# Relative-position attention layer: the stores of the relative products move from SP's queue to ACT's, behind ACT's copies

## The reference

```python
q, k, v = ...                       # (8, 16, 512, 16), from layernorm(x) and from the context
QEr  = jnp.einsum('bhsd,ld->bhsl', q, Er_s)      # 512 x 512 for each head
padded   = jnp.pad(QEr, ((0, 0), (0, 0), (0, 0), (1, 0)))
Srel     = padded.reshape(B, H, C + 1, R)[:, :, 1:, :]
attn = (QK + Srel) / math.sqrt(dh)
attn = jnp.where(causal[None, None], attn, -jnp.inf)
attn = jax.nn.softmax(attn, axis=-1)
out  = jnp.einsum('bhqk,bhkd->bhqd', attn, v)
x = x + out
```

## Time and profile before

| | us |
|---|---|
| median of 3 runs | 4367.12 |
| lowest and highest | 4364.86 and 4370.69 |
| the profiled execution's own time | 4376.57 |
| its span | 4374.7 |
| busy: PE, DVE, ACT, POOL | 3537.7, 2556.5, 1760.6, 1149.3 |
| this layer's attention, first transfer to last score | about 2210 to 3125 |

### The profile page before, as it was taken

How to read it: one execution, slowest core, us unless ns; L and a number is a source line. 1 busy time by engine, 2 the same in 40 slices (tenths; PEclk the granted TensorE clock), 3 DMA queues, 4 the chain that set the end, 5 groups by cost and what they waited for, 6 DMA issues and landing times. The chain is left out here.

```text
span 4374.7 us, 68566 instructions
## 1 busy us (share of the span) xinstructions
PE 3537.7 (81%) x18821; PEld 1770.6 (40%) x18821; DVE 2556.5 (58%) x7436; ACT 1760.6 (40%) x2506; POOL 1149.3 (26%) x1239
## 2 busy tenths in 40 slices
PE   3999999897399899969957777776538999996697
PEld 1343343343133333336634444444313434335465
DVE  4665665776487777853125555555666666663531
ACT  0454455443044344441125545555433445552111
POOL 2334430001445444401022222221222212201132
PEclk7999999898699999979978888888658999996799
DMA  5543540001454344310048888888332432313133
GB/s 109 84 68 62 77 73 12 19 1 42 72 93 83 74 83 78 73 46 0 0 104 223 231 231 220 232 232 229 125 56 35 56 49 35 49 16 107 46 99 68
DMA packets 211868, 392.82 MB, mean 90 GB/s; under 512 B 24624, under 2 KB 76688, under 8 KB 211360
## 3 DMA queue, kind: packets, MB, share of 16 engines
q1 hardware_dynamic: 205344, 379.99, 39.9%
q0 software_dynamic: 6144, 8.39, 1.1%
HBM read 189.88 MB, written 96.47 MB: 65 GB/s over the span
## 5 line engine op out<-in xcount | busy, mean ns | idle before, releaser
L424 DVE CUSTOM_DVE_ANT_0 A_sums<-A_p_ps,A_bias 128x512 bf16<-128x512 f32 x1536 | 1006.1, 687 | 411.8 <-PE A_p_ps L270 389.4
L497 ACT ACTIVATE A_probs<-A_p_ps 128x1024 f32<-128x1024 f32 x640 | 654.3, 1024 | 613.0 <-PE A_p_ps L289 591.0
L270 PE MATMUL A_p_ps<-A_k_stack,A_q_stack 96*128 96x512 bf16 x1536 | 512.0, 390 | 106.5 <-DVE A_nmax L424 96.4
L284 PE MATMUL A_p_ps<-A_q_stack,A_k_stack 99*128 99x512 bf16 x1536 | 461.9, 382 | 0.1
L299 PE MATMUL A_oT_ps<-A_probs,A_v_aug 128*17 128x512 f32 x3072 | 407.0, 602 | 3.2 <-ACT A_probs L497 2.4
L1082 DVE CUSTOM_DVE_ANT_0 A_scores<-A_qk_ps,A_rel_in 128x384 f32<-128x384 f32 (+3 forms) x512 | 232.7, 486 | 215.6 <-POOL A_rel_in L1151 114.8
L990 PE MATMUL A_t_ps<-ident,A_scores 128*128 128x128 f32 x1280 | 225.3, 315 | 134.5 <-DVE A_probsT L1072 124.7
L270 PEld LDWEIGHTS A_p_ps<-A_k_stack,A_q_stack 96*128 96x128 bf16 x1536 | 135.6, 98 | 486.1 <-DVE A_nmax L424 387.6
L289 PE MATMUL A_p_ps<-A_biasT,ident_bf 128*128 128x512 bf16 x1024 | 307.4, 381 | 0.0
L1072 DVE COPY A_probsT<-A_t_ps 128x1024 f32<-128x1024 f32 (+3 forms) x256 | 210.5, 822 | 120.7 <-PE A_t_ps L990 114.1
L1133 ACT ACTIVATE A_scores<-A_scores,A_nmax 128x384 f32<-128x384 f32 (+3 forms) x512 | 257.9, 555 | 48.5 <-DVE A_nmax L1082 48.3
(11 more groups left out here) (356 smaller groups left out, 5901.6 us busy)
## 6 DMA issues: line engine op xcount, KB each, us to landing
A_k_stack<-A_parts SPq DMA_DIRECT2D x192, 256.0 KB, 8.9
A_q_stack<-A_parts SPq DMA_DIRECT2D x192, 256.0 KB, 9.2
A_rel_dram<-A_rel_out SPq DMA_DIRECT2D x64, 512.0 KB, 4.9
A_rel_in<-A_rel_dram SPq DMA_DIRECT2D x64, 512.0 KB
A_rel_dram<-A_rel_out SPq DMA_DIRECT2D x64, 384.0 KB, 4.4
A_rel_in<-A_rel_dram SPq DMA_DIRECT2D x64, 384.0 KB, 4.4
A_ctxT<-in_ctxT SPq DMA_DIRECT2D x32, 512.0 KB, 12.7
A_mask_in<-in_mask SPq DMA_DIRECT2D x64, 256.0 KB, 3.5
```

Source lines behind the costliest of these rows:

```text
L270: nc.tensor.matmul(p1_ps[i % 2][:, :], q_stack[0:KS, a_par, j * GH + i, t * P:(t + 1) * P], k_stack[0:KS, a_par, j * GH + i, :], start=Tru ...
L284: last = nc.tensor.matmul(p2_ps[half][:, i % 2, :], k_stack[:, par, j * GH + i, kb * P:(kb + 1) * P], q_stack[:, par, j * GH + i, :], star ...
L424: nc.vector.tensor_tensor_reduce(out=sums[:, i % NX, :], in0=p1_ps[i % 2][:, :], in1=bias[:, t, :], scale=-1.0, scalar=3.4028235e38, op0=A ...
L497: nc.scalar.activation(dst, src, ACT.Exp).then_inc(exp_done, 1)
```

## The change

The function that issued both stores of a step on SP is gone; a function of the same waits and the same transfer issues one store on ACT, at the end of each position, behind the exponentials. SP's frame keeps loads, stack and context transfers in the order they had. No buffer, semaphore, size or other order changes.

```diff
+        def act_rel_store(act, b, a, h):
+            _, _, n = block_of(a)
+            act.wait_ge(rel_copied, (b * STEPS + a) * 2 + h + 1)
+            if later(b * STEPS + a - NI + 1):
+                act.wait_ge(rel_loaded[a % NI][h], (b * (STEPS // NI) + a // NI) * 16)
+            act.dma_start(bass.AP(rel_dram, a % NI * RING + h * RING // 2, [[2 * n, P], [1, 2 * n]]),
+                          rel_out[a % NO][:, 2 * h * n:(2 * h + 2) * n]).then_inc(rel_stored[a % NO][h], 16)
...
                         nc.scalar.activation(scores[u % NP][:, i, 0:n], scores[u % NP][:, i, 0:n], ACT.Exp,
                                              bias=nmax[:, u % NP, i:i + 1], scale=-1.0).then_inc(exp_done, 1)
+                if has(b, a):
+                    act_rel_store(act, b, a, half)
...
-        def sp_rel_store(sp, b, a):
-            _, _, n = block_of(a)
-            for h in range(2):
-                sp.wait_ge(rel_copied, (b * STEPS + a) * 2 + h + 1)
-                if later(b * STEPS + a - NI + 1):
-                    sp.wait_ge(rel_loaded[a % NI][h], (b * (STEPS // NI) + a // NI) * 16)
-                sp.dma_start(bass.AP(rel_dram, a % NI * RING + h * RING // 2, [[2 * n, P], [1, 2 * n]]),
-                             rel_out[a % NO][:, 2 * h * n:(2 * h + 2) * n]).then_inc(rel_stored[a % NO][h], 16)
...
                 if has(b, s + LEAD - 1):
                     sp_rel_load(sp, b, s + LEAD - 1)
-                if has(b, s + LEAD):
-                    sp_rel_store(sp, b, s + LEAD)
                 if after and s in (0, 1):
```

## The result

| | before | after |
|---|---|---|
| median of 4 runs, us | 4365.99 (4363.15 to 4370.69) | 4222.56 (4217.24 to 4229.22) |
| profiled execution's own time, us | 4376.57 | 4223.41 |
| its span, us | 4374.7 | 4221.6 |
| granted TensorE clock over the span | 0.895 | 0.915 |
| the eight frames of the layer, us | 837.6 | 686.7 |

The changed kernel takes 0.9671 of the time [0.9654, 0.9688]. In the profiled executions 150.9 of the 153.1 us of span come out of the eight frames of this layer, so the rest of the program needs no look.

A forecast was written before the change was run, and what follows sets the result against it. SP's in-order chain of load, store and landing was taken to bound the kernel, as long as a step (6.8 us). Terms -50 - 20 - 10 + 18 = -62 us gave 4305 us at the median; range 4255 to 4390.

The forecast's parts named there:

- the term for PE (context and clock): PE's 25.9 us of waits for the next context, 10 us taken as gained; nothing counted for a faster PE clock.
- the mask: DVE's 74.9 us of waits for the mask, without the layer's filling: 50 us taken as gained.
- ACT's issues: ACT issues 256 stores; bounds nothing and 154 us, a third of 57 us taken as cost: +18 us.
- the root: DVE's waits for POOL's root (L1142), 27.9 us in 6 waits: 20 us taken as gained.
- The three terms: DVE's waits for mask and root and PE's waits for the context, forecast at -50, -20 and -10 us.
- The first rival: DMA transfers are the bound, so early loads only wait inside the DMA engines: 4367 us, chance 0.10.
- the slower rival: ACT becomes the bound, all 256 issues on the path at 0.60 us: +51 us, 4418 us, chance 0.16.
- the context: PE's waits for the next context's transfer in SP's queue, 25.9 us in 6 waits: 10 us taken as gained.
- I count nothing for that: Fewer waits may raise PE's granted clock, 0.82 to 0.87 in these frames; sized at nothing.
- the ceiling: All three waits go, up to 97 us in six frames and about 11 in the last: 4259 us, chance 0.10.
- a sign to look for: SP's waits for stores to land fall from 470.7 us to below 100; SP waits for DVE's scores instead.
- The other signs: Mask waits about 25 us, root below 10, steady frame about 99 at share above 0.90, PE's copy waits up under 20.

The follow-up runs named there:

- the spare stores: Changed kernel with every store issued a second time, to a DRAM buffer that nothing reads: 4299.36 us, ratio 0.9847.
- the early context in the kernel before: Kernel before, stores on SP, with the next context's transfer moved from step 6 to step 5, ahead of the stack transfers: 4379.7 us, ratio 1.0027.
- the one-step kernel: Changed kernel whose loads also wait until DVE has scored one step before their own, instead of four: 4503.3 us, ratio 1.0308.

## Why the prediction was right and wrong

The forecast gave 62 us, the eight profiled frames gave 150.9, 89 more. Of these, 40 are the term for PE (context and clock), 23 the mask, 18 ACT's issues, 1 the root, and 6 other waits that the sum left out. The three terms at their full bounds, 74.9 + 27.9 + 25.9 = 128.7 us, would have given 4238 us, still above what was measured.

**Right: the mechanism and its sign.** The chain load, landing, next store, landing held the layer. Undoing it on one queue gives 131 of the 143 us, and a longer wait in front of the load takes it all back. The first rival (transfers are the bound) fell with this. The Trainium skill ("DMA: Bandwidth & Descriptors", section "Issuing engines are not separate DMA queues") says that transfers started by different engines run on the same 16 DMA engines. The runs agree as far as they go, since one queue carried 276 GB/s in a frame for which two queues show 274. It also says that starting them on several engines saves only the issuing time. That does not describe this change; what was saved is the time that ready stores stood behind a waiting load.

**Right: the root.** -20 forecast, -21.0 measured. The direction has its reason; that it came to within 1 us is luck, since no row stood behind taking 20 of 27.9.

**Right: ACT is not the bound**, the slower rival. Its point of decision was 0.31 us uncovered per issue. 256 further issues cost 0.04 us each, at most 0.10.

**Mis-sized: the mask.** -50 forecast, -73.1 measured. The step that failed is to count only 15 of the 40 us of waits behind the stack transfers as gained. The 40 was sound, though 6.72 us was not the longest wait: the trace has seven, one in each of frames 0 to 6, 41.9 us in all and up to 7.83 us. That 25 of the 40 would stay was not. I argued that the engines were full there because their share was 0.90 to 1.09, where they moved 183 to 281 GB/s. Over the same 26.6 us they moved 227 GB/s before, 277 after and 326 with the spare stores, so over the burst they were not full. An average lead of 7.2 us more, with no lead under 8.9 us, left 1.8 us of mask waits. I had also expected up to 12 us more, from one step.

**Mis-sized: the context, and the line "I count nothing for that", said of the clock.** This is the largest step that failed. -10 forecast, -50.4 measured. PE's wait of 25.9 us went altogether, and DVE's waits for products of PE fell by 38.5 and 11.9 us. PE's busy time fell by 55.8 us with the same matmuls, as this group shows, before and then after (busy us, mean ns, idle before it):

```profile
L927 PE MATMUL A_front_ps<-A_ctxT,A_wk 128*128 128x512 f32 x48 | 33.7, 841 | 25.9 <-DMA A_ctxT<-in_ctxT 25.9
```

```profile
L927 PE MATMUL A_front_ps<-A_ctxT,A_wk 128*128 128x512 f32 x48 | 24.3, 631 | 0.1
```

How the 50 us split between a context that comes in time and a faster PE is not settled: no run holds the clock and moves the context. That the products can come earlier at an unchanged clock is shown by the early context in the kernel before (85.4 to 33.3 us, clock 0.896 over the span against 0.895), but there DVE was held up by masks at the same time (121.1 us), so PE had more time to get ahead.

**Mis-sized: ACT's issues.** +18 forecast, and nothing of it is seen: PE's waits for ACT's copies go from 4.0 to 7.1 us, and DVE's waits have no term for it. No run isolates the 256 issues, so 0 is the reading of these waits and not a measurement. Of the two reasons given for the lower bound, waits in front of copies and exponentials that still run, it is the second: the issue runs under exponentials that were already handed over. I had expected the store some 2 us after the copy, and it leaves 0.1 us after it. Placed where nothing covers it, it cost 21 us.

**Wrong: the ceiling.** "A steady frame holds 0.85 x 108.2 = 92 us of DMA work" is the step that put 4222 out of the range. It made frames under 92 us impossible, and they take 80.9 to 94.1. The same bytes need (232 GB/s x 106.0 us) / 359 GB/s = 68.5 us at the rate of the spare stores' run. The six frames gave 118.5 us instead of at most 97. The ceiling also left out frame 0, which gave 20.0 us, from 104.2 to 84.2; the last frame gave 12.4 for the 11 allowed.

**Wrong: a sign to look for.** SP's waits for landings were to fall below 100 us with waits for DVE's scores in their place; 427.6 us remain, and 15.8 us are for scores. By this sign a theory that holds would have been refuted. What a queue's wait means depends on whether it is ahead of or behind its consumers. The other signs came: the root below 10 us, the share of a steady frame at 0.90 to 0.99, PE's waits for copies up by less than 20.

The terms as measured, -73.1 - 21.0 - 38.5 - 11.9 and others -6.4, make the 150.9 us of the profiled layer.

## What to carry to other kernels

For each transfer on a busy queue, measure the time from when its data is ready to its issue, and from its issue to its first use; a store that stands ready behind a waiting load is worth moving, and swapping two blocks on the same queue may be nearly all of it. Do not take a DMA share as a capacity: turn it into GB/s and set it beside the highest rate that a run with such transfers shows. And put an issue behind instructions whose conditions are already met, so that it runs under them.

## What the runs showed of the hardware

An issue on ACT takes 0.33 us at the median and ran under an exponential, 0.14 us after the copy before it ended, though it stands behind two exponentials in the program: the queue side of ACT is ahead of its arithmetic. Placed directly behind the copy it left a gap of 0.62 us. The DMA engines moved 359 GB/s in a frame at a share of 1.05, and 357 at 0.93, so nearly equal rates can have different shares. PE's granted clock was higher where there were fewer waits: 0.82 to 0.87 in the frames of the earlier trace rows, 0.90 to 0.96 in those shown after, and 0.77 in the one-step kernel's frame of 127 us.
